# Recurrent block with a routed feed-forward on one core: the second layer norm's aggregate one step later, four dummy products left out, the transpose of h2 behind the expert job

## The chip, the cores and the metric

The kernel runs on one core of one Trainium2 chip. The metric is the device time of one execution in microseconds (us). Three runs of the kernel before took 710.07, 710.91 and 711.07; their median is 710.91.

## The reference, cut to what matters

Eight sequences of 512 tokens with 128 features pass through two blocks.

```python
h = layernorm(x) * (1 + ca) + sa
x = x + ga * mixer(h)          # scan over 512 steps, below
h = layernorm(x) * (1 + cb) + sb
x = x + gb * ffn(h)            # each token goes to the expert with the largest gate

def step(carry, inp):          # mixer
    h_ssm = silu(h_ssm @ A.T + bxt)
    y_ssm = h_ssm @ Cw.T + Cb + dxt
    r = sigmoid(i_r + h_r); z = sigmoid(i_z + h_z); n = tanh(i_n + r * h_n)
    h_rnn = (1.0 - z) * n + z * h_rnn
    y_rnn = h_rnn @ proj_w.T + proj_b
    return (h_ssm, h_rnn), gxt[:, :1] * y_ssm + gxt[:, 1:2] * y_rnn
```

The feed-forward has eight experts, each relu(x @ w1 + b1) @ w2 + b2 with 512 hidden units. All arithmetic is in float32.

## The kernel before

**Tiles and steps.** The 512 steps of the recurrence are cut into 32 tiles c of 16 steps t; a tile holds 16 steps of 8 sequences, so 128 tokens, one per partition. Every engine runs one list of steps g = 16 c + t, and in each of them first its share of the recurrence, then work of other tiles: while the recurrence works on tile c, the engines finish tile c-1 (outputs of the mixer, residual, second layer norm, routing, placing of its rows), prepare tile c+1 (first layer norm, its transpose, the input products), and run expert jobs of earlier groups of tiles. The tiles fall into five groups of 6, 7, 7, 6 and 5; the last tile is done densely. After step 511 there is a tail, in which the engines run the steps of tiles 32 and later without the recurrence.

**The recurrence.** TensorE makes the r product from u (`rs_bank`), then the n and z products from h_ring (`nz_bank`), later in the step the product of the state space and the product of mw for the next step (`carried`, L1297). ScalarE makes r_fac (L787), s_ring (L790), v_fac (L793) and n_fac (L795); VectorE makes the scan (L1122), mw (L1126), u (L1130) and h_ring (L1133). The scan needs r_fac, and r_fac needs u of the step before.

**Around the recurrence.** The step function of VectorE (L1111) puts behind h_ring, in this order: the mixing of tile c-1 at t=2 to 5 (gates, mix, mixg, x), its second layer norm (`post`, L896) from t=6, routing at t=10 to 15, the tables of the dispatch (`lay_out`, L1047, one instruction a step in tiles 7, 14, 21 and 27, t=2 to 11), the first layer norm of a later tile (`pre`, L891), then what leaves the expert jobs' banks: a ReLU of the second hidden bank (L1197) or the addition of the bias into y_sb (L1209); at last the final products. Each engine takes its instructions strictly in order.

**Layer norm in four parts** (L873). Part 0 is bn_stats (L877), part 1 bn_aggr (L880), part 2 xc = (x - mean) * scale (L883), part 3 the result, xc * rstd + shift (L888). Between parts 1 and 3 GpSimd makes rstd in two instructions, an addition of eps (L649) and a power (L651). GpSimd's step function (L701) takes the rstd of the first norm, then at t=6 the rstd of the second norm, then loads of rows for the last group by indirect DMA (L690, at fixed steps; two of them at t=6 of tile 32), then scatters and gathers. `pre_steps` (L253) says at which step the four parts of the first norm run; tiles 1 and 2 have a line of their own there.

**Expert jobs.** A slot is a block of 128 rows of one expert. Its jobs are X (transpose of the rows), A and C (hidden products, chunks 0/1 and 2/3), D and B (output products), each a product of 128 x 128 x 128 in float32. `schedule` (L164) places them by hand-written room: at most `ROOM` = 2 jobs a step, less what `ENDED` and `NEXT` take for tile work. The second of each pair of A and C uses the bank `hid_bank[1]`, whose ReLU is done by VectorE in the step of the job or by ScalarE at the end of it (in the next step for a job in second place).

**TensorE's step** (L1418) is: recurrence products, `tile_work` (L1366; at t=7 the transpose of h1, at t=9 the transpose of h2, which waits for h2), expert jobs, then `hold_clock` (L1311) if there is room, then the state space and `carried`. `hold_clock` is a dummy product of 128 or 256 columns into `hid_bank[1]`, and so waits for every ReLU of that bank that is issued:

```python
ge(eng, relu_b_ready, count_of("AC", u, place))
mm(hid_bank[1][:, 0:width], ident, w_sb[:, W_MOD:W_MOD + width], start=True, stop=True)
```

ScalarE copies the transposes out of PSUM in the step in which TensorE makes them (h1T L736, h2T L817).

**SyncE's queue** loads each slot's expert weights (L583, after reading the expert's number, L582), loads its rows (L589) and stores its results (L600, L597), in the order of the steps.

Of the kernel before, what the change touches and what calls it, by code (L numbers as in the profile page):

```python
# [96 lines left out]
ROOM = 2  # L97
# [8 lines left out]
def taken(u):  # L106

    return (ENDED[u % T] if u >= T else 0) + (NEXT[u % T] if u < (NT - 1) * T else 0)
# [55 lines left out]
def schedule():  # L164

    at, on_act, ready, act_ops, dve_used = {}, set(), {}, {}, {}

    def may(event, u, place):
        return event in ready and ready[event] <= (u, place)

    def ok(unit, u, place, first):
        kind, n, h = unit
        new = n == first
        if kind == "X":
            return new or may(("C", n - 1, 0), u, place)
        if kind == "A":
            return may(("X", n, 0), u, place) and (new or (may(("C", n - 1, h), u, place) and ("D", n - 1, h) in ready))  # L180
        if kind == "C":
            return may(("A", n, h), u, place) and ("A", n, 1) in ready and (new or ("B", n - 1, h) in ready)
        if kind == "D":
            return may(("A", n, h), u, place) and (new or may(("B", n - 1, 1), u, place))
        return may(("C", n, h), u, place) and ("D", n, 1) in ready

    def dve_room(u):
        return 270 if u // T < DVE_EARLY.get(u % T, 0) else DVE_ROOM[u % T]

    def home(unit, u, place):  # L190


        kind, n, h = unit
        if kind == "D" or unit[0::2] == ("B", 0):
            return "PE"
        if (kind == "B" or kind != "X" and h) and dve_used.get(u, 0) + DVE_COST[kind == "B"] <= dve_room(u):
            return "DVE"
        if kind != "B" and act_ops.get(u + (place > 0), 0) < ACT_ROOM[(u + (place > 0)) % T]:
            return "ACT"
        return None  # L200

    u = 0
    for k in range(NG - 1):
        first, end = SLOT0[k], SLOT0[k + 1]
        head = {"X": [], "A": [], "B": [], "C": [], "D": []}
        for unit in order_of_units(k):
            head[unit[0]].append(unit)
        u = max(rows_at(k) + 4, u)
        while any(head.values()) and u < NT * T:
            place = 0  # L210
            while place < ROOM - taken(u):
                for kind in PICK[place > 0]:
                    unit = head[kind][0] if head[kind] else None
                    where = home(unit, u, place) if unit and ok(unit, u, place, first) else None
                    if where:
                        break
                else:
                    break
                head[kind].pop(0)
                at.setdefault(u, []).append(unit)  # L220
                ready[unit] = (u, place + 1)
                if where == "ACT":
                    act_ops[u + (place > 0)] = act_ops.get(u + (place > 0), 0) + 1
                    ready[unit] = (u + (place > 0) + 1, 0)
                    if unit[2]:
                        on_act.add(unit)
                if where == "DVE":
                    dve_used[u] = dve_used.get(u, 0) + DVE_COST[kind == "B"]
                    ready[unit] = (u + 1, 1)
                place += 1  # L230
            u += 1


    def room(u):
        return 3 if u < NT * T + T else 2

    u, used = NT * T, 0
    for k in range(NG):
        if rows_at(k) + 4 > u:
            u, used = rows_at(k) + 4, 0  # L240
        for i, what in enumerate(order_of_units(k)):
            if what in ready:
                continue
            if i == 1:
                u, used = u + 1, 0
            while used >= room(u):
                u, used = u + 1, 0
            at.setdefault(u, []).append(what)
            used += 1
    return at, on_act  # L250


def pre_steps():  # L253

    pre, rstd = {}, {}
    for j in range(1, NT):
        at = (j - 1) * T
        steps = (at + 2, at + 3, at + 5, at + 6) if j < 3 else (at - 7, at - 6, at, at + 1)
        for part, u in enumerate(steps):
            pre.setdefault(u, []).append((j, part))  # L260
        rstd.setdefault(steps[1], []).append(j)
    return pre, rstd


PRE_AT, RSTD_AT = pre_steps()
UNITS, ON_ACT = schedule()
Y_STEP = {SLOT_OF[i]: u for u, what in UNITS.items() for kind, i, second in what
          if kind == "B" and second and i in SLOT_OF}
Y_AT = {u: n for n, u in Y_STEP.items()}
# [28 lines left out]
def adaln_kernel(nc, x, silu_in, weights, ssm_weights, w1, b1, w2, b2, col_bias, bias_a, bias_b,  # L298
                 bias_const, const, out):
    ctx = ExitStack()  # L300
    with ctx:
# [46 lines left out]
        u = sb("u", [P, 2, B])  # L348
# [143 lines left out]
        def exists(tile):  # L492

            return 0 <= tile < NT
# [135 lines left out]
        def _(eng):  # L630
# [70 lines left out]
            def step(u, c, q, t):  # L701

                for tile in RSTD_AT.get(u, []):
                    rstd(tile, mv1, ve1, rs1, ln1_step, ve1_done, rs1_ready)
                if t == 6 and exists(c - 1):
                    rstd(c - 1, mv2, ve2, rs2, ln2_step, ve2_done, rs2_ready)
                for n in range(SLOT0[NG - 1], NSLOT):
                    if u == max(rows_at(NG - 1) + 1, X_STEP[n] - 12):
                        load_rows(n)
                for j in range(NS):  # L710
                    if u == scatter_at(j):
                        ge(eng, h_ready, min(u, NT * T))
                        scatter(j)
                    if u == GATHER_AT[j]:
                        ge(eng, h_ready, min(u, NT * T))
                        gather(j)
# [148 lines left out]
        def _(eng):  # L865
# [30 lines left out]
            def post(j, part):  # L896
                if part == 3 and j >= RING:
                    k = group_of_tile(j - RING)
                    ge(eng, scattered[k % 3], 16 * sum(SIZE[i] for i in range(k % 3, k + 1, 3)))
                layer_norm(j, st2, mv2, rs2, xc2, mod_cb, mod_sb, h2_ring[:, j % RING, :], ln2_step, rs2_ready, h2_ready,  # L900
                           part)
# [209 lines left out]
            def step(g, c, q, t):  # L1111
# [24 lines left out]
                if exists(j):  # L1136
                    xs = x_sb[:, j * P:(j + 1) * P]
                    if t == 2:
                        ge(eng, gates_raw, j + 1)
                        nc.vector.tensor_scalar(g_sb[:, :], g_raw[:, :], 0.5, 0.5, ALU.mult,  # L1140
                                                ALU.add).then_inc(gates_ready, 1)
                    if t == 3:
                        ge(eng, yr_ready, j + 1)
                        nc.vector.scalar_tensor_tensor(out=mix[:, :], in0=work[:, Y_S:Y_S + P],
                                                       scalar=g_sb[:, 0:1], in1=yr_sb[:, :],
                                                       op0=ALU.mult, op1=ALU.add).then_inc(mix_ready, 1)
                    if t == 4:
                        ge(eng, mix_ready, j + 1)
                        nc.vector.tensor_tensor(mixg[:, :], mix[:, :], mod_ga, ALU.mult).then_inc(mixg_done, 1)
                    if t == 5:  # L1150
                        ge(eng, mixg_done, j + 1)
                        nc.vector.tensor_tensor(xs, mixg[:, :], xs, ALU.add).then_inc(x1_ready, 1)
                    if t == 6:
                        ge(eng, x1_ready, j + 1)
                        post(j, 0)
                        post(j, 1)
                    if t in (7, 8):
                        post(j, t - 5)
                    if 10 <= t <= 15:
                        route(j, 1 - q, t)  # L1160
                if c == NT and 5 <= t < 5 + INDEX_STEPS:
# [73 lines left out]
        def _(eng):  # L1235
# [182 lines left out]
            def step(g, c, q, t):  # L1418
# [24 lines left out]
                    mm(z_cols(q, t), wg[:, WG_Z:WG_Z + P] if g else w_sb[:, W_HH + P:W_HH + 2 * P], h_ring[:, pq, pt, :],  # L1443
                       start=False, stop=True, skip_group_check=True).then_inc(z_ready, 1)

                tile_work(c, q, t, g)
                units = UNITS.get(g, [])
                for kind, n, second in units:
                    unit(kind, n, second)
                if exists(c):  # L1450
                    room = ROOM - taken(g) - len(units)
                    if room == 2:
                        hold_clock(g, len(units), 2 * P)
                    if room == 1:
                        hold_clock(g, len(units), P)
                    if g == 0:
                        ge(eng, rn_ready, 2)
                    ge(eng, hs_ready, g)
                    state_space(g, pq, pt).then_inc(s_ready, 1)
                    if exists((g + 1) // T):  # L1460
                        carried(g + 1)
# [56 lines left out]
```

## Time and profile before

| | |
|---|---|
| Median of three runs | 710.91 us |
| Profiled execution | 709.89 us, span 708.0 us |
| TensorE busy, matmul and weight load | 97% and 91% |
| VectorE, ScalarE, GpSimd busy | 76%, 60%, 18% |
| TensorE's mean granted clock | 0.997 |
| Chain that ended last, by engine | TensorE 92%, VectorE 3%, DMA 2% |
| Chain, by output | rs_bank 33%, nz_bank 23%, hid_bank_b 11%, work 11% |

The span runs from the first to the last instruction of the program; the execution's time has some more around it. A busy share counts the time in which at least one instruction of the engine was open; matmuls are pipelined, so TensorE's share says little about how much more it could do. In a timeline each row has the start, the time, the engine, the line, the operation, output and inputs, the shape and a count; like instructions that follow each other are merged; in brackets stands the idle time before the instruction and what ended it. PE is TensorE, DVE VectorE, ACT ScalarE, POOL GpSimd, SP SyncE.

### The profile page before, as it was taken

How to read it: one execution, taken by the hardware profiler on the slowest of the kernel's cores; microseconds unless marked ns; L12 is line 12 of the kernel's file. 1: busy time of each engine (PE TensorE's matmuls, PEld its weight loads, DVE VectorE, ACT ScalarE, POOL GpSimd, SP SyncE). 2: the span in 40 equal slices, each digit the busy share in tenths (PEclk: the TensorE clock that was granted, in tenths of full speed). 3: DMA queues.
4: the chain of work that ended last, by engine and by line, in shares of the span. 5: the costliest groups of instructions: out<-in, count | busy, mean ns of one | idle time of the engine just before them, and what ended most of it. 6: DMA issues, size and time to landing. Idle time of an engine off the chain costs nothing.

```text
span 708.0 us, 35792 instructions
## 1 busy us (share of the span) xinstructions
PE 689.0 (97%) x13884; PEld 646.8 (91%) x13884; DVE 538.9 (76%) x3233; ACT 428.2 (60%) x2678; POOL 127.7 (18%) x221
## 2 busy tenths in 40 slices
PE   8999999999999999999999999999999999998796
PEld 5899999999999999999999999999999999997695
DVE  4777777787787777888887788878787878877465
ACT  4555555556766676566666765766667666664342
POOL 4011111111110111111111112111111112213432
PEclk9999999999999999999999999999999999999999
DMA  8916000604432000063321001632210343224731
GB/s 305 344 60 229 7 7 7 241 9 165 158 118 84 20 15 11 14 229 141 105 84 55 22 19 55 234 137 97 80 38 15 135 165 108 99 100 170 278 123 52
DMA packets 45468, 76.72 MB, mean 108 GB/s; under 512 B 6284, under 2 KB 27090, under 8 KB 45170
## 3 DMA queue, kind: packets, MB, share of 16 engines
q1 hardware_dynamic: 40914, 68.33, 27.0%
q0 software_dynamic: 2368, 4.85, 2.4%
q8 instruction: 110, 1.80, 1.1%
q10 hardware_dynamic: 2016, 1.25, 0.6%
q14 instruction: 60, 0.49, 0.2%
HBM read 14.31 MB, written 21.04 MB: 50 GB/s over the span
## 4 chain that ended last, share of the span: by engine, by line
PE 92%; DVE 3%; DMA 2%; issue 1%; ACT 1%; SPq 1%; POOLq 0%; DVEq 0%
PE rs_bank L1239 33%; PE nz_bank L1239 23%; PE hid_bank_b L1239 11%; PE work L1239 11%; PE y_bank L1239 7%; PE hid_bank_a L1239 7%; DMA yg<-rows,pos 1%; DMA rows<-y_sb 1%; DMA out<-o_sb 0%; SPq L582 0%; DVE u L1130 0%; ACT v_fac L793 0%; DVE mw L1126 0%; DVE y_sb L1209 0%; DVE hid_b L1197 0%
## 5 line engine op out<-in xcount | busy, mean ns | idle before, releaser
L1239 PE MATMUL nz_bank<-h_ring,wg 128*64 128x16 f32 x4088 | 207.2, 211 | 0.0
L787 ACT ACTIVATE r_fac<-rs_bank 128x8 f32<-128x8 f32 x512 | 91.3, 178 | 176.9 <-PE rs_bank L1239 171.2
L1239 PE MATMUL rs_bank<-s_ring,ws_sb 128*64 128x128 f32 x1024 | 195.0, 272 | 0.0
L1239 PEld LDWEIGHTS nz_bank<-h_ring,wg 128*64 128x64 f32 x4088 | 161.1, 136 | 1.3
L1239 PE MATMUL rs_bank<-mw,wg 128*64 128x8 f32 x2044 | 148.5, 202 | 0.0
L1239 PE MATMUL rs_bank<-u,wg 128*64 128x8 f32 x2044 | 142.0, 206 | 0.1
L1122 DVE TENSOR_TENSOR_SCAN nz_bank<-r_fac,nz_bank 128x16 f32<-128x16 f32 x512 | 99.6, 195 | 53.1 <-ACT r_fac L787 33.0
L1239 PEld LDWEIGHTS rs_bank<-s_ring,ws_sb 128*64 128x64 f32 x1024 | 127.3, 136 | 9.2
L1126 DVE SCALAR_TENSOR_TENSOR mw<-v_fac,h_ring 128x8 f32<-128x8 f32 x512 | 85.9, 168 | 54.5
L1239 PEld LDWEIGHTS rs_bank<-mw,wg 128*64 128x64 f32 x2044 | 105.0, 135 | 17.3 <-DVE mw L1126 3.5
L793 ACT ACTIVATE v_fac<-nz_bank 128x8 f32<-128x8 f32 x512 | 90.7, 177 | 40.6
L1239 PEld LDWEIGHTS rs_bank<-u,wg 128*64 128x64 f32 x2044 | 103.1, 135 | 1.4
L1133 DVE SCALAR_TENSOR_TENSOR h_ring<-mw,u 128x8 f32<-128x8 f32 x512 | 85.3, 167 | 17.4
L795 ACT ACTIVATE n_fac<-nz_bank 128x8 f32<-128x8 f32 x512 | 90.7, 177 | 3.1 <-DVE nz_bank L1122 0.6
L1130 DVE SCALAR_TENSOR_TENSOR u<-v_fac,n_fac 128x8 f32<-128x8 f32 x512 | 85.5, 167 | 3.6 <-ACT n_fac L795 0.5
L790 ACT ACTIVATE s_ring<-rs_bank 64x8 f32<-64x8 f32 x512 | 81.0, 158 | 0.4 <-PE rs_bank L1239 0.4
L1239 PE MATMUL hid_bank_b<-w_sb,const_sb 128*64 128x128 f32 (+1 forms) x608 | 76.8, 322 | 2.3 <-ACT hid_b L775 2.3
L665 POOL DMA_INDIRECT rows<-h_ring,pos x31 | 31.7, 1022 | 244.3 <-DVE h_ring L1133 241.6
L779 ACT ACTIVATE hid_a<-hid_bank_a,wx 128x128 f32<-128x128 f32 x132 | 48.5, 368 | 17.6 <-PE hid_bank_a L1239 15.1
L1239 PE MATMUL hid_bank_a<-xT,wx 128*64 128x128 f32 x528 | 55.3, 283 | 0.6 <-issue 0.4
L1239 PE MATMUL hid_bank_b<-xT,wx 128*64 128x128 f32 x528 | 54.4, 280 | 1.3 <-DVE hid_b L1197 1.3
L1239 PE MATMUL y_bank<-wx,hid_a 128*64 128x128 f32 x528 | 54.1, 279 | 0.8 <-DVE y_sb L1209 0.8
(179 smaller groups left out, 1084.6 us busy)
## 6 DMA issues: line engine op xcount, KB each, us to landing
wx<-w_all SPq DMA_DIRECT2D x66, 578.0 KB, 3.9
rows<-zeros SPq DMA_DIRECT2D x3, 4096.0 KB, 14.5
w_all<-in_w SPq DMA_DIRECT2D x2, 2048.0 KB, 15.8
xs_sb<-rows SPq DMA_DIRECT2D x54, 64.0 KB, 2.9
rows<-y_sb SPq DMA_DIRECT2D x54, 64.0 KB, 1.6
x_sb<-in_x SPq DMA_DIRECT2D x1, 1920.0 KB, 9.7
out<-o_sb SPq DMA_DIRECT2D x19, 64.0 KB
out<-o_sb ACTq DMA_DIRECT2D x13, 64.0 KB
```

Source lines behind the costliest of these rows:

```text
L665: nc.gpsimd.indirect_dma_start(rows[k % 3].ap(), index(pos, j), h2_ring[:, j % RING, :], None).then_inc(scattered[k % 3], 16)
L779: nc.scalar.activation(hid_a[:, h, :], hid_bank[0][:, 0:P], ACT.Relu, bias=bias1(i, 2 * h)).then_inc(relu_a_ready, 1)
L787: nc.scalar.activation(r_fac[:, k, :, 1], r_cols(q, t), ACT.Tanh, scale=0.5).then_inc(rn_ready, 1)
L790: nc.scalar.activation(s_ring[0:SSM, pq, pt, 0:B], s_cols(g - 1), ACT.Silu).then_inc(hs_ready, 1)
L793: nc.scalar.activation(v_fac[:, k, :], z_cols(q, t), ACT.Tanh, scale=-0.5).then_inc(sig_ready, 1)
L795: nc.scalar.activation(n_fac[:, k, :], n_pairs(q, t)[:, :, 1], ACT.Tanh).then_inc(tanh_ready, 1)
L1122: nc.vector.tensor_tensor_scan(pairs, r_fac[:, k, :, :].rearrange("p b k -> p (b k)"), pairs, 0.0, ALU.mult, ALU.add).then_inc(pre_n_ready, 1)
L1126: nc.vector.scalar_tensor_tensor(out=mw[:, k, :], in0=v_fac[:, k, :], scalar=1.0, in1=h_ring[:, pq, pt, :], op0=ALU.subtract, op1=ALU.mult ...
L1130: nc.vector.scalar_tensor_tensor(out=u[:, k, :], in0=v_fac[:, k, :], scalar=1.0, in1=n_fac[:, k, :], op0=ALU.add, op1=ALU.mult).then_inc(u ...
L1133: nc.vector.scalar_tensor_tensor(out=h_ring[:, q, t, :], in0=mw[:, k, :], scalar=-0.5, in1=u[:, k, :], op0=ALU.mult, op1=ALU.add).then_inc ...
L1239: last = nc.tensor.matmul(out[c:c + COLS], weights[:, c:c + COLS], moving, start=start, stop=stop, skip_group_check=skip_group_check)
```

## The change

The second layer norm's bn_aggr moves from t=6 to t=7, where xc already stands, and GpSimd's rstd of that norm from t=6 to t=7. `schedule` also returns the set of steps at which a ReLU of the second hidden bank is open, and in these steps TensorE makes no dummy product. At t=9 the expert jobs come ahead of `tile_work`, that is of the transpose of h2. The last two parts of the first layer norm of tiles 1 and 2 run one step earlier.

```diff
@@ schedule
+                if kind in "AC" and unit[2]:
+                    relu_open.update(range(u, ready[unit][0] + ready[unit][1]))
...
-    return at, on_act
+    return at, on_act, relu_open
@@ pre_steps
-        steps = (at + 2, at + 3, at + 5, at + 6) if j < 3 else (at - 7, at - 6, at, at + 1)
+        steps = (at + 2, at + 3, at + 4, at + 5) if j < 3 else (at - 7, at - 6, at, at + 1)
@@ GpSimd, step
-                if t == 6 and exists(c - 1):
+                if t == 7 and exists(c - 1):
                     rstd(c - 1, mv2, ve2, rs2, ln2_step, ve2_done, rs2_ready)
@@ VectorE, step
                     if t == 6:
                         ge(eng, x1_ready, j + 1)
                         post(j, 0)
+                    if t == 7:
                         post(j, 1)
-                    if t in (7, 8):
-                        post(j, t - 5)
+                        post(j, 2)
+                    if t == 8:
+                        post(j, 3)
@@ TensorE, step
-                tile_work(c, q, t, g)
+                if t != 9:
+                    tile_work(c, q, t, g)
                 units = UNITS.get(g, [])
                 for kind, n, second in units:
                     unit(kind, n, second)
+                if t == 9:
+                    tile_work(c, q, t, g)
                 if exists(c):
-                    room = ROOM - taken(g) - len(units)
+                    room = 0 if g in RELU_OPEN else ROOM - taken(g) - len(units)
```

## Rows read from the trace of the kernel before

**Rows 1.** All h_ring writes (L1133): count, min/median/max ns, first and last start.

```profile
L1133 DVE SCALAR_TENSOR_TENSOR h_ring<-mw,u x512: 166/166/170, 12.2 to 639.0; 128x8 f32<-128x8 f32 x171
```

**Rows 2.** Timeline of VectorE, tile 9, t=6 to t=9: start us, us, line, operation.

```profile
195.17 0.17 DVE L1133 SCALAR_TENSOR_TENSOR h_ring<-mw,u 128x8 f32<-128x8 f32 x1
...
195.57 0.18 DVE L880 BATCH_NORM_AGGREGATE mv<-st 128x2 f32<-128x6 f32 x1
195.67 0.32 DVE L1197 TENSOR_SCALAR hid_b<-hid_bank_b,wx 128x128 f32<-128x128 f32 x1
195.91 0.18 DVE L1122 TENSOR_TENSOR_SCAN nz_bank<-r_fac,nz_bank 128x16 f32<-128x16 f32 x1
...
196.53 0.17 DVE L1133 SCALAR_TENSOR_TENSOR h_ring<-mw,u 128x8 f32<-128x8 f32 x1
...
197.74 0.17 DVE L1133 SCALAR_TENSOR_TENSOR h_ring<-mw,u 128x8 f32<-128x8 f32 x1
197.83 0.35 DVE L888 SCALAR_TENSOR_TENSOR h_ring<-xc,rs,mod 128x128 f32<-128x128 f32 x1
...
198.95 0.17 DVE L1133 SCALAR_TENSOR_TENSOR h_ring<-mw,u 128x8 f32<-128x8 f32 x1
...
199.23 0.34 DVE L1197 TENSOR_SCALAR hid_b<-hid_bank_b,wx 128x128 f32<-128x128 f32 x1
...
200.19 0.17 DVE L1133 SCALAR_TENSOR_TENSOR h_ring<-mw,u 128x8 f32<-128x8 f32 x1
```

**Rows 3.** Waits, whole span: engine and line, waited for: us, times, longest.

```profile
PE hid_bank_b L1239 <- ACT hid_b L775: 2.3, 4, 0.8
```

**Rows 4.** Timeline of VectorE, tile 11, t=6 and t=7.

```profile
234.26 0.17 DVE L1133 SCALAR_TENSOR_TENSOR h_ring<-mw,u 128x8 f32<-128x8 f32 x1
...
235.57 0.17 DVE L1133 SCALAR_TENSOR_TENSOR h_ring<-mw,u 128x8 f32<-128x8 f32 x1
...
237.38 0.17 DVE L1133 SCALAR_TENSOR_TENSOR h_ring<-mw,u 128x8 f32<-128x8 f32 x1
```

**Rows 5.** Timeline of VectorE, tile 31, t=9.

```profile
631.68 0.17 DVE L1133 SCALAR_TENSOR_TENSOR h_ring<-mw,u 128x8 f32<-128x8 f32 x1
...
632.96 0.17 DVE L1133 SCALAR_TENSOR_TENSOR h_ring<-mw,u 128x8 f32<-128x8 f32 x1
```

**Rows 6.** Timeline of VectorE, tile 7, t=7.

```profile
157.86 0.26 DVE L1068 TENSOR_TENSOR ended<-passed,end_slot 128x104 f32<-128x104 f32 x1
```

**Rows 7.** Timeline of GpSimd, tile 9, t=6.

```profile
195.84 0.18 POOL L649 TENSOR_TENSOR ve<-mv,eps 128x1 f32<-128x1 f32 x1 [2.82 <-DVE mv L880]
196.10 0.57 POOL L651 TENSOR_TENSOR rs<-ve,half 128x1 f32<-128x1 f32 x1
```

**Rows 8.** Timeline of GpSimd, tile 1, t=6.

```profile
40.22 0.26 POOL L649 TENSOR_TENSOR ve<-mv,eps 128x1 f32<-128x1 f32 x1 [2.89 <-DVE mv L880]
```

**Rows 9.** Timeline of TensorE, tile 9, t=9.

```profile
198.23 0.44 PE L1239 MATMUL work<-const_sb,h_ring 128*64 128x128 f32 x4
```

**Rows 10.** Timeline of ScalarE, tile 9, t=10.

```profile
199.34 0.18 ACT L787 ACTIVATE r_fac<-rs_bank 128x8 f32<-128x8 f32 x1 [0.36 <-PE rs_bank L1239]
```

**Rows 11.** Timeline of VectorE, tile 1, t=6 and the end of t=7.

```profile
39.55 0.17 DVE L1133 SCALAR_TENSOR_TENSOR h_ring<-mw,u 128x8 f32<-128x8 f32 x1
...
42.50 0.17 DVE L1133 SCALAR_TENSOR_TENSOR h_ring<-mw,u 128x8 f32<-128x8 f32 x1
```

**Rows 12.** Timeline of GpSimd, tile 32, t=6.

```profile
649.00 0.94 POOL L690 DMA_INDIRECT xs_sb<-rows,x_index  x1 [0.30 <-issue]
```

**Rows 13.** Timeline of VectorE, tile 32, t=13.

```profile
653.07 0.28 DVE L1209 TENSOR_TENSOR y_sb<-y_bank,wx 128x128 f32<-128x128 f32 x1
```

**Rows 14.** Timeline of SyncE's queue, tail.

```profile
655.38 0.52 SPq L600 DMA_DIRECT2D rows<-y_sb  x1
```

**Rows 15.** Timeline of TensorE, tail.

```profile
667.86 0.44 PE L1239 MATMUL rs_bank<-const_sb,xs_sb 128*64 128x128 f32 x4 [3.53 <-DMA xs_sb<-rows,x_index]
```

**Rows 16.** Stretch: its us, each engine's busy us, TensorE's granted clock, DMA.

```profile
669.40:672.80 3.40, 3.40 (x36) 3.40 (x34) 0.87 (x4) 1.00 (x3) 2.49 (x4) 0.51 0.94 345
```

More of the change, by code:

```diff
@@ L164, in schedule @@
 def schedule():
-    at, on_act, ready, act_ops, dve_used = {}, set(), {}, {}, {}
+    at, on_act, ready, act_ops, dve_used, relu_open = {}, set(), {}, {}, {}, set()
     def may(event, u, place):
@@ L265 @@
 PRE_AT, RSTD_AT = pre_steps()
-UNITS, ON_ACT = schedule()
+UNITS, ON_ACT, RELU_OPEN = schedule()
 Y_STEP = {SLOT_OF[i]: u for u, what in UNITS.items() for kind, i, second in what
```

## The prediction

> **What bounds the kernel.** I read the page first, and its TensorE share (in the table above) is misleading: dummy products fill that engine. What sets the time is a recurrence of 512 steps, each of which writes one h_ring. The row of all h_ring writes puts them between 12.2 and 639.0 us [rows 1]: 626.8 us for 511 steps, 1.227 us each. So the second view is the timeline of VectorE around single steps. There the reader is to see the distance from one h_ring to the next: 197.74 to 198.95 is 1.21 us, 196.53 to 197.74 is 1.21 us [rows 2], and I take 1.205 as the floor. 511 floors are 615.8 us, so 11.0 us of the recurrence is excess, and that is all that the change can win before the tail (the last 69 us, behind the last h_ring). I then looked for which steps hold the excess. Step numbers t run from 0 to 15 in each of 32 tiles c; a distance is put to the step that begins it.
>
> At **t=6** VectorE has bn_stats, bn_aggr and, in many tiles, one more instruction between h_ring and the next scan. In tile 9 the scan starts at 195.91, 0.74 behind h_ring at 195.17, and the step takes 1.36 [rows 2]; without that 0.155 of excess it would start 0.58 behind. That is the free window of a step. At **t=7** of four tiles TensorE's dummy product waits for the ReLU that still reads its bank: 2.3 us in four waits, the longest 0.8 [rows 3]; the step takes 1.81 (235.57 to 237.38) [rows 4]. At **t=9** each step is a little long: 1.24 in tile 9 [rows 2], 1.28 in tile 31 [rows 5].
>
> **The change part by part.**
>
> *The dummy products.* The set of steps with an open ReLU has 149 members, but only four of them still had room for a dummy: t=7 of tiles 11, 18, 25 and 31. The other 148 dummies stay. Each of three steps returns 1.81 - 1.205 = 0.605. The fourth dummy is twice as wide and its wait is 0.8 where the others leave (2.3 - 0.8)/3 = 0.5, so I take 0.9. Sum 3 x 0.605 + 0.9 = **-2.7 us**. What is late next: ScalarE's ReLU and the copy of h1's transpose, which it has in other tiles' t=7 in the same number at 1.21 (tile 9 [rows 2]). So nothing is left of the stall, and at worst 0.1 in each.
>
> *The aggregate leaves t=6.* It starts 0.40 behind h_ring (195.57) and the ReLU 0.50 (195.67); without it the ReLU can start 0.28 behind, as behind bn_stats at t=9 (199.23 against 198.95) [rows 2]. ReLU to scan is 0.24 (195.67 to 195.91), so the scan is free at 0.52, inside 0.58. Eight tiles have a ReLU there: 8 x 0.155 = **-1.24**. Eight have the y_sb addition instead, at 1.31 (234.26 to 235.57) [rows 4]: 8 x 0.105 = **-0.84**. The other tiles from 2 to 31 lose nothing there today, but for the four with a table step of the dispatch (7, 14, 21, 27), for which I take 0.1 each.
>
> *The aggregate arrives at t=7.* There stands only xc. The aggregate starts 0.09 behind h_ring and takes 0.18; xc needs its result and starts at 0.30; the scan is free 0.24 to 0.28 later, at 0.54 to 0.58. This just fits: 0 taken, and 0.05 in each of 31 tiles as the bad end. In the four dispatch tiles the table product stands behind xc, 0.26 long [rows 6]. Its cost lies between 0 and 0.26; I take 0.2, nearer to the row, since the window is full. Four times 0.1 - 0.2 is **+0.4**.
>
> *The reciprocal root on GpSimd.* It follows the aggregate, which now comes 0.9 later (1.205 + 0.09 - 0.40). Its two instructions run from 195.84 to 196.67 [rows 7], 0.92 behind the aggregate's end (195.75). From t=7 that is 0.27 + 0.92 = 1.19 behind h_ring, and h2 wants it at 1.205 + 0.09 = 1.295 (it starts 0.09 behind its h_ring, 197.83 against 197.74). It is hidden, with 0.1 to spare. But the first of the two now lies beside xc, and where it lay beside another such product, in tile 1, it took 0.26 and not 0.18 [rows 8]. Then h2 starts some 0.03 late, which only the tiles without work ahead of the transpose feel: **+0.2** in all. The Trainium skill, GPSIMD Engine Reference, section Key points, says that GpSimd shares its SBUF interfaces with VectorE and contends with instructions of two SBUF inputs, as xc is; that speaks against this move, and by that the trace agrees. By the rule the sum is as it stands; if rule and row did not hold it would be 0.2 better.
>
> *The transpose behind the expert job at t=9.* h2 ends at 197.83 + 0.35 = 198.18 and the transposes start at 198.23 [rows 9]: TensorE waits for h2, and r_fac of the next step is late with it. With a job of four such products first (0.44 with its drain, as this row), the wait is covered. 22 of the tiles 8 to 31 have a job at t=9; 14 and 21 have none and keep theirs, as do 1 to 7. Five tiles return 1.24 - 1.205, seventeen 1.28 - 1.205 (from tile 13 on h2 has one more wait): **-1.45**. What moves with it: ScalarE's copy of the transpose, and what it does behind it; ScalarE idles 0.36 before r_fac at 199.34 [rows 10], nearly a whole job, and a job's start-to-start is less than its 0.44, so I take no cost. The bounds are 0 (ScalarE takes the place of the wait) and -1.45.
>
> *First layer norm of tiles 1 and 2.* Its last two parts come one step sooner, so TensorE finds h1 ready at t=7, and t=6 is relieved. In tile 1 t=6 and t=7 take 42.50 - 39.55 = 2.95 [rows 11], 0.54 over two floors. Tile 0 has the same pair, and I take as much: **-1.08**. The parts arrive at t=4 and t=5 beside one other 128x128 instruction, and two fit (0.28 + 0.24).
>
> *The tail.* One queue is passed: on GpSimd the two loads of rows of step t=6 of tile 32 now stand ahead of the root, each 0.94 with 0.30 before it [rows 12], 2.5 us at most. They start before the root's old turn, so I take 1.6 of it for h2 of the last tile, and for VectorE, which waits for the root in order with all that is queued behind; the two loads come sooner. I cost this at nothing, for two covers. SyncE stores the y_sb of 653.07 [rows 13] only at 655.38 [rows 14], its queue being behind: 653.07 + 0.28 + 1.6 is still ahead of that. And TensorE waits 3.53 us for rows at 667.86 [rows 15], which are gated by that queue and not by h2. With the covers gone it costs 1.6.
>
> Sum: -2.7 - 1.24 - 0.84 + 0.4 + 0.2 - 1.45 - 1.08 = **-6.7 us**, of the 11.0. The profiled execution took 709.89 (span 708.0 and 1.9 around it), so 703.2; the median shown, 710.91, is 1.0 above it, so **704.2**.
>
> **The rivals.**
>
> *The tail gains.* Today's wait of 3.53 is followed by the granted clock at 0.51 from 669.40 to 672.80 [rows 16], the lower level, 1.2 GHz, for 3.4 us: 1.7 us lost. If the late h2 pushes 1.5 us of TensorE's work into that wait, 2.0 are left of it, and no row shows whether 2.0 is enough to lower the clock. If not, 704.2 - 1.7 = 702.5. The Trainium skill, TensorE: Matmul & The Clock Gate, section on the HAM clock gate, says that recent activity sets the clock; by that the gain is possible, and the trace agrees as far as it goes.
>
> *t=7 is the new t=6.* Aggregate and xc overfill it by 0.05 in 31 tiles: 1.55, so 705.75; for it speaks that the fit above has no slack, against it that the aggregate is short.
>
> *The root is late, and the kernel slower.* h2 can slip from 0.09 to 0.58 - 0.26 = 0.32 before it holds the scan of t=8. Past that, each 0.1 costs 31 x 0.1 = 3.1, and from 0.22 past it the kernel is slower than before. With both instructions at twice their length (0.75 more) it would be 0.75 - 0.10 - 0.23 = 0.42 past: 13.0, so 717.2. Against it: the contention seen is 0.08.
>
> *Half of it does nothing.* If t=6 and t=9 are long for another reason (TensorE's own work), only the dummies and tiles 0 and 1 count, -3.8, with the losses of 0.6: 707.7. Against it: the scans at t=6 stand right behind VectorE's own instructions.
>
> **How the numbers follow.** Forecast 0.52, tail gain 0.20, overfull t=7 0.20, the half case 0.04, the late root 0.04 (0.01 of it within 0.2% of before). The range takes in the forecast, the tail gain with 0.5 of its unknowns (702.0) and the overfull t=7 with half of the t=9 term missing (706.4). 0.2% (1.4 us) is about what a measurement of this kernel can tell from no change: faster 0.96, the same 0.01, slower 0.03.
>
> **What would show it.** Right: no wait of a dummy for a ReLU; steps t=6 and t=7 at 1.205 in tiles like 9 and 11, t=7 at 1.4 in the four dispatch tiles; t=9 at 1.205 in tiles with a job; the last h_ring near 632.3. Wrong: scans behind xc later than 0.58 after h_ring, h2 later than 0.12, or a tail longer than 69 us.

## The result and the profile after

The changed kernel took 703.26 us in the median of four runs (701.33 to 703.70), against 710.99 of before: a ratio of 0.9885, 95% interval 0.9866 to 0.9903. Five runs more gave 702.04 (experiment e8). The forecast was 704.2, the range 702.0 to 706.4. The profiled execution took 701.33 (span 699.5), 8.6 less than the profiled one of before.

The page of the changed kernel gives the busy times and the chain; TensorE has 16 records less than before (13884), four for each of the four dummy products, and its share of the chain is 94%:

```profile
PE 683.9 (98%) x13868; PEld 641.9 (92%) x13868; DVE 536.6 (77%) x3233; ACT 426.1 (61%) x2678; POOL 129.0 (18%) x221
...
PE 94%; DMA 2%; DVE 1%; issue 1%; POOL 0%; SPq 0%; ACT 0%; POOLq 0%; DVEq 0%
```

The row of all h_ring writes, which stands against [rows 1]:

```profile
L1135 DVE SCALAR_TENSOR_TENSOR h_ring<-mw,u x512: 166/166/170, 11.6 to 632.4; 128x8 f32<-128x8 f32 x171
```

The last h_ring comes at 632.4 and not at 639.0, 6.6 us sooner. Of that 0.5 is the start (11.6 and not 12.2, before the change acts), so 6.1 are the recurrence. The other 2.0 are the tail: 699.5 - 632.4 = 67.1, before 708.0 - 639.0 = 69.0.

VectorE in tile 9, t=6 to t=9, against [rows 2]:

```profile
193.76 0.17 DVE L1135 SCALAR_TENSOR_TENSOR h_ring<-mw,u 128x8 f32<-128x8 f32 x1
...
194.04 0.33 DVE L1201 TENSOR_SCALAR hid_b<-hid_bank_b,wx 128x128 f32<-128x128 f32 x1
194.32 0.19 DVE L1124 TENSOR_TENSOR_SCAN nz_bank<-r_fac,nz_bank 128x16 f32<-128x16 f32 x1
...
194.96 0.17 DVE L1135 SCALAR_TENSOR_TENSOR h_ring<-mw,u 128x8 f32<-128x8 f32 x1
195.05 0.17 DVE L882 BATCH_NORM_AGGREGATE mv<-st 128x2 f32<-128x6 f32 x1
195.25 0.35 DVE L885 SCALAR_TENSOR_TENSOR xc<-x_sb,mv,mod 128x128 f32<-128x128 f32 x1
195.53 0.20 DVE L1124 TENSOR_TENSOR_SCAN nz_bank<-r_fac,nz_bank 128x16 f32<-128x16 f32 x1
...
196.17 0.17 DVE L1135 SCALAR_TENSOR_TENSOR h_ring<-mw,u 128x8 f32<-128x8 f32 x1
196.41 0.35 DVE L890 SCALAR_TENSOR_TENSOR h_ring<-xc,rs,mod 128x128 f32<-128x128 f32 x1
196.68 0.28 DVE L1213 TENSOR_TENSOR y_sb<-y_bank,wx 128x128 f32<-128x128 f32 x1
196.88 0.18 DVE L1124 TENSOR_TENSOR_SCAN nz_bank<-r_fac,nz_bank 128x16 f32<-128x16 f32 x1
...
197.51 0.17 DVE L1135 SCALAR_TENSOR_TENSOR h_ring<-mw,u 128x8 f32<-128x8 f32 x1
...
198.71 0.17 DVE L1135 SCALAR_TENSOR_TENSOR h_ring<-mw,u 128x8 f32<-128x8 f32 x1
```

At t=6 the ReLU starts 0.28 behind h_ring, as forecast, the scan 0.56 (forecast 0.52, and free up to 0.58), and the step takes 1.20 (1.36 before). At t=7 aggregate, xc and scan start 0.09, 0.29 and 0.57 behind; the step takes 1.21. At t=9, behind a job, 1.20 (1.24 before). But t=8 takes 1.34 and took 1.21: h2 starts 0.24 behind its h_ring and not 0.09, the y_sb addition comes behind it, and the scan only 0.71 behind. Tile 11's t=7, against [rows 4], is 1.20, and no dummy's wait for a ReLU [rows 3] is left; tile 7's t=7, a dispatch tile, is 1.40:

```profile
233.78 0.17 DVE L1135 SCALAR_TENSOR_TENSOR h_ring<-mw,u 128x8 f32<-128x8 f32 x1
...
234.98 0.17 DVE L1135 SCALAR_TENSOR_TENSOR h_ring<-mw,u 128x8 f32<-128x8 f32 x1
```

```profile
156.03 0.17 DVE L1135 SCALAR_TENSOR_TENSOR h_ring<-mw,u 128x8 f32<-128x8 f32 x1
...
156.63 0.25 DVE L1070 TENSOR_TENSOR ended<-passed,end_slot 128x104 f32<-128x104 f32 x1
156.81 0.18 DVE L1124 TENSOR_TENSOR_SCAN nz_bank<-r_fac,nz_bank 128x16 f32<-128x16 f32 x1
...
157.43 0.17 DVE L1135 SCALAR_TENSOR_TENSOR h_ring<-mw,u 128x8 f32<-128x8 f32 x1
```

Why h2 was late in tile 9 stands on GpSimd, against [rows 7]; below it tile 8, with its xc on VectorE in the second fence:

```profile
175.99 0.18 POOL L651 TENSOR_TENSOR ve<-mv,eps 128x1 f32<-128x1 f32 x1 [3.77 <-DVE mv L882]
176.25 0.57 POOL L653 TENSOR_TENSOR rs<-ve,half 128x1 f32<-128x1 f32 x1
...
195.31 0.34 POOL L651 TENSOR_TENSOR ve<-mv,eps 128x1 f32<-128x1 f32 x1 [3.69 <-DVE mv L882]
195.73 0.57 POOL L653 TENSOR_TENSOR rs<-ve,half 128x1 f32<-128x1 f32 x1
```

```profile
175.93 0.38 DVE L885 SCALAR_TENSOR_TENSOR xc<-x_sb,mv,mod 128x128 f32<-128x128 f32 x1
```

In tile 9 the addition of eps took 0.34 and xc 0.35; in tile 8, at the same place in the step, the addition took 0.18 and xc 0.38. Every tile shows one of the two. I call a root behind an addition of 0.34 a late root; in this execution tiles 3, 6, 9, 10, 11 and 29 have one. Tiles 3 and 6, with no job at t=9, lose 0.16 there, tiles 9 and 29, with a y_sb at t=8, lose 0.13 and 0.15; 10 and 11 lose nothing, since the job ahead of the transpose covers it.

In the tail TensorE's wait for rows, against [rows 15], is 0.78 and not 3.53, and its granted clock from 663.0 to 669.0 is 1.00, the 2.4 GHz level, where it was 0.51 behind the wait [rows 16]. The first fence has the wait, the second the stretch: its length, busy times, clock:

```profile
660.71 0.44 PE L1243 MATMUL rs_bank<-const_sb,xs_sb 128*64 128x128 f32 x4 [0.78 <-DMA xs_sb<-rows,x_index]
```

```profile
663.00:669.00 6.00, 6.00 (x107) 5.54 (x104) 3.72 (x13) 2.68 (x9) 4.67 (x5) 1.00 0.84 284
```

### The profile page after: what moved, and what is told of

Same layout as the page of the kernel before. It is cut to its first block, busy times and chain, and to the rows that moved or that the text cites. A ratio compares the mean times of both kernels' runs of the same rounds, so it can differ in the third digit from the quotient of the medians.

```text
span 699.5 us, 35760 instructions
## 1 busy us (share of the span) xinstructions
PE 683.9 (98%) x13868; PEld 641.9 (92%) x13868; DVE 536.6 (77%) x3233; ACT 426.1 (61%) x2678; POOL 129.0 (18%) x221
## 3 DMA queue, kind: packets, MB, share of 16 engines
q10 hardware_dynamic: 2016, 1.25, 0.6%
## 4 chain that ended last, share of the span: by engine, by line
PE 94%; DMA 2%; DVE 1%; issue 1%; POOL 0%; SPq 0%; ACT 0%; POOLq 0%; DVEq 0%
PE rs_bank L1243 34%; PE nz_bank L1243 23%; PE hid_bank_b L1243 12%; PE work L1243 11%; PE y_bank L1243 8%; PE hid_bank_a L1243 7%; DMA xs_sb<-rows,x_index 1%; DMA rows<-y_sb 1%; DMA out<-o_sb 1%; DVE fin_g L1219 0%; POOL xs_sb L692 0%; DVE hid_b L1201 0%; POOL yg L681 0%; SPq L584 0%; DVE prob L1014 0%
## 5 line engine op out<-in xcount | busy, mean ns | idle before, releaser
L1243 PE MATMUL rs_bank<-mw,wg 128*64 128x8 f32 x2044 | 146.4, 202 | 0.0
L1243 PE MATMUL rs_bank<-u,wg 128*64 128x8 f32 x2044 | 140.0, 206 | 0.1
L1243 PEld LDWEIGHTS rs_bank<-mw,wg 128*64 128x64 f32 x2044 | 103.0, 135 | 18.6 <-DVE mw L1128 4.3
L1243 PE MATMUL hid_bank_b<-w_sb,const_sb 128*64 128x128 f32 (+1 forms) x592 | 74.8, 322 | 0.0
```

The costliest lines, as they stand in the source:

```text
L1243: last = nc.tensor.matmul(out[c:c + COLS], weights[:, c:c + COLS], moving, start=start, stop=stop, skip_group_check=skip_group_check)
```

## The experiments

All were timed against the kernel before on the same chip; its median was 710.35 in e1 to e4, 710.24 in e5 to e8, 710.80 in e9 to e11 and 710.45 in e12. From e5 on each account opens with the median in us, the range of the runs, and the ratio to before with its 95% interval. Steps, last h_ring and tail are read from the one profiled execution of each kernel.

### The four parts, each alone on the kernel before

```diff
e1  +                    room = 0 if g in RELU_OPEN else ROOM - taken(g) - len(units)
e2  +                if t == 7 and exists(c - 1): rstd(c - 1, mv2, ...)      # GpSimd
    +                    if t == 7: post(j, 1); post(j, 2)                  # VectorE
e3  +                if t == 9: tile_work(c, q, t, g)                       # behind the units
e4  +        steps = (at + 2, at + 3, at + 4, at + 5) if j < 3 else ...
```

> The kernel before with the four dummy products left out and nothing else. Theory (the terms of the change add up): t=7 of tiles 11, 18, 25 and 31 falls to about 1.21 us, the last h_ring comes 2.6 us sooner, the tail stays at 69.0 us, the time falls by 2.6 us (ratio 0.9963). Rival (the dummies held TensorE's clock or only hid a wait of the ReLU itself): less than 1.5 us, with t=7 of these tiles above 1.4 us. Rival for the tail (its 2.0 us gain belongs to the phase in which the tail begins, not to one part): the tail is shorter than 68 us here too.

> The kernel before with the second norm's aggregate and its reciprocal root moved to t=7, and nothing else. Theory (the root behind two loads of rows shortens the tail; the second product against GpSimd's addition costs some tiles): t=6 gives 2.5 us, t=7 of the four dispatch tiles takes back 0.8, six tiles with a late root (ve 0.34 and not 0.18 us long) take back about 0.9, so the last h_ring comes 0.8 us sooner; the tail falls from 69.0 to about 67 us; together 2.8 us less (ratio 0.996). Rival (the tail's gain is not of this part): tail 69.0 us, together 0.8 us less (ratio 0.999). Rival for the late roots (they come with the other parts): no ve longer than 0.20 us in tiles 2 to 31, 1.7 us less in the recurrence.

> The kernel before with the expert jobs ahead of the transpose at t=9, and nothing else. Theory (terms add up): t=9 of 22 tiles falls from 1.24 to 1.28 us to about 1.21 us, the last h_ring comes 1.25 us sooner, the tail stays at 69.0 us, the time falls by 1.25 us (ratio 0.998). Rival (ScalarE's copy of the transpose takes the place of the wait): t=9 stays above 1.23 us in these tiles, under 0.4 us in all.

> The kernel before with the last two parts of the first layer norm of tiles 1 and 2 one step sooner, and nothing else. Theory: t=6 and t=7 of tiles 0 and 1 fall by 1.0 us in all, but for what the aggregate at t=6 costs in tile 1 (0.15), so 0.9 us; nothing later changes, tail 69.0 us (ratio 0.9987). Rival (the pair of steps is long because of the aggregate alone): under 0.4 us.

| | median us | range us | ratio | last h_ring | tail |
|---|---|---|---|---|---|
| e1 dummies | 707.58 | 706.31 to 709.64 | 0.9965 [0.9953, 0.9977] | 635.7 | 70.9 |
| e2 aggregate | 707.90 | 705.88 to 712.78 | 0.9972 [0.9956, 0.9989] | 639.9 | 71.1 |
| e3 transpose | 708.57 | 705.54 to 709.69 | 0.9972 [0.9960, 0.9984] | 637.5 | 69.8 |
| e4 first norm | 709.33 | 708.28 to 710.34 | 0.9984 [0.9975, 0.9994] | 636.7 | 70.7 |

(The last two columns are of the profiled execution.) In e1 the four steps return 0.61, 0.61, 0.61 and 0.82, 2.66 together. In e3 t=9 falls by 1.17 in all, in e4 t=6 and t=7 of tiles 0 and 1 by 1.02. In the steps that they touch these three parts are what they were expected to be, and their rivals fall. In medians the four parts alone gain 2.77, 2.45, 1.78 and 1.02 us, 8.0 together, against 7.7 and 8.2 for the whole change. No tail is shorter than 69 in the four profiled executions, but one execution each does not tell whose part the tail's gain is: e2, for one, has five runs of twelve with a mean clock above 0.997, which no run of before has.

e2 is the odd one. Its profiled execution took 712.78, longer than before: t=6 gave 2.7 and t=7 took 0.75, but t=8 and t=9 took 3.0 more. 25 tiles had the long addition, 19 of them a late h2. Tile 2 in e2 (GpSimd at t=7, VectorE from t=7 to the end of t=9):

```profile
60.10 0.34 POOL L649 TENSOR_TENSOR ve<-mv,eps 128x1 f32<-128x1 f32 x1 [3.46 <-DVE mv L880]
60.52 0.57 POOL L651 TENSOR_TENSOR rs<-ve,half 128x1 f32<-128x1 f32 x1
```

```profile
59.75 0.17 DVE L1133 SCALAR_TENSOR_TENSOR h_ring<-mw,u 128x8 f32<-128x8 f32 x1
60.05 0.35 DVE L883 SCALAR_TENSOR_TENSOR xc<-x_sb,mv,mod 128x128 f32<-128x128 f32 x1
...
60.96 0.17 DVE L1133 SCALAR_TENSOR_TENSOR h_ring<-mw,u 128x8 f32<-128x8 f32 x1
61.21 0.35 DVE L888 SCALAR_TENSOR_TENSOR h_ring<-xc,rs,mod 128x128 f32<-128x128 f32 x1
...
62.17 0.17 DVE L1133 SCALAR_TENSOR_TENSOR h_ring<-mw,u 128x8 f32<-128x8 f32 x1
...
63.57 0.17 DVE L1133 SCALAR_TENSOR_TENSOR h_ring<-mw,u 128x8 f32<-128x8 f32 x1
```

h2 starts 0.25 behind, and t=9 takes 1.40. The twelve runs lie 6.9 us apart (e4's 2.1). The late root is not fixed to tiles: here it falls on 25, in the changed kernel's profile on six, and e8 shows others for that same kernel. In the whole change e3's part hides most of what e2's part costs.

### The late root

e5 and e6 leave out the addition and take the root straight from the variance, so GpSimd has one instruction (and the output differs); e9 makes the addition twice; e8 is the changed kernel unaltered.

```diff
e5 on the changed kernel, e6 on e2:
+                if mv is mv2:
+                    nc.gpsimd.tensor_tensor(rs, mv[:, 1:2], half, ALU.pow); return
e9 on the changed kernel:
+                    nc.gpsimd.tensor_tensor(rs, mv[:, 1:2], eps, ALU.add)
                     nc.gpsimd.tensor_tensor(ve, mv[:, 1:2], eps, ALU.add)
                     nc.gpsimd.tensor_tensor(rs, ve, half, ALU.pow)
```

> The changed kernel, with the root of the second norm taken straight from the variance: GpSimd's addition of eps is left out (the output differs by that). Theory (the late roots come from this addition beside xc): no h2 starts later than 0.13 us behind its h_ring, t=9 of tiles 3 and 6 and t=8 of tiles 9 and 29 return to 1.205 to 1.25 us, the recurrence is 0.6 us shorter than in the profiled execution of the changed kernel. Rival (any instruction of GpSimd beside xc is lengthened, so the power instead): the power takes 0.73 us and not 0.57, xc 0.35, h2 still starts in time since the root ends at about 1.1 us, so the same time, but the power shows the contention. Rival (the late h2 has another cause): some h2 at 0.24 us or more.

> The kernel before with the aggregate and the root moved to t=7 as in e2, and the addition of eps left out for the second norm. Theory (late roots make e2's loss at t=8 and t=9 and its spread of 6.9 us between executions): t=8 and t=9 as before (1.205 and 1.24 to 1.28 us), so the recurrence is 1.9 us shorter than before instead of 1.5 longer; the runs lie within 3.5 us of each other, and their median is at least 0.5 us under e2's 707.9. Rival (the spread comes from the tail): a spread of 6 us or more here too, with all h2 in time.

> The changed kernel once more, unaltered, to see what differs between executions. Theory (two things differ: which tiles have a late root, and how long the tail's wait for rows is): the steps t=6 and t=7 are the same within 0.02 us in every tile, the tiles with ve of 0.34 us are others than 3, 6, 9, 10, 11 and 29, the tail lies between 67 and 71 us, the runs lie 3 us apart. Rival: the same six tiles again, and a tail of 67.1 us.

> The changed kernel with GpSimd's addition of eps made twice for the second norm, the first time into rs. The root ends 0.26 us later, at 1.44 us behind the h_ring of t=7 or at 1.60 where the addition beside xc is long, so h2 starts at about 0.33 to 0.50 us in every tile. Theory (past 0.32 us h2 holds the scan of t=8, and each 0.1 us past it costs that in the tile): t=8 is 0.05 to 0.20 us longer in all tiles, t=9 0.24 us longer in the nine tiles without a job, the recurrence 3 to 6 us longer. Rival (a late root is hidden but at the transpose and y_sb): t=8 is 1.205 us but in tiles 9, 16, 23 and 29, the recurrence 1.5 to 3 us longer.

**e5**: 700.25 (699.67 to 702.49), 0.9866 [0.9849, 0.9883]. No h2 is late, and the four steps return to between 1.21 and 1.25. Yet its first rival is right about the contention: the power, now beside xc, is the one that is long. The two rows of e5's roots, first norm and second (count, min/median/max ns):

```profile
L656 POOL TENSOR_TENSOR rs<-ve,half x32: 550/552/672, 6.4 to 588.0; 128x1 f32<-128x1 f32 x32
L652 POOL TENSOR_TENSOR rs<-mv,half x32: 549/725/732, 39.9 to 642.3; 128x1 f32<-128x1 f32 x32
```

The first norm's power takes 0.55, the second's, beside xc, 0.73 in most tiles. It is the overlap that costs, not the addition; without the addition the root is early enough to bear it. The 0.6 us expected shows at t=8 and t=9 (0.53 less, and 0.25 less at t=7), but 0.7 more, spread thinly over all other steps, leaves the recurrence of this execution as it was. In medians e5 lies 1.8 under the unaltered kernel of the same rounds (e8).

**e6**: 706.49 (705.59 to 710.43), 0.9959 [0.9945, 0.9973]. t=8 and t=9 are as before to 0.03 us in all, the recurrence is 1.5 shorter where e2's was 1.5 longer, and the median is 1.4 under e2's. So e2 lost its time by the late roots. The spread, 4.8, lies between the 3.5 of the theory and the 6 of the rival: part of it is not the late roots'.

**e8**: 702.04 (701.86 to 704.67), 0.9896 [0.9879, 0.9913]. t=6 and t=7 are as in the first execution to 0.03, and 17 tiles have the long addition, of which only 6, 10, 11 and 29 had it before; tail 67.4. So the tiles differ by execution.

**e9**: 711.26 (710.52 to 713.53), 1.0012 [1.0001, 1.0022]. Tile 2 in e9, t=7 to t=9: the root is late enough to hold the scan:

```profile
59.06 0.17 DVE L1142 SCALAR_TENSOR_TENSOR h_ring<-mw,u 128x8 f32<-128x8 f32 x1
59.35 0.35 DVE L892 SCALAR_TENSOR_TENSOR xc<-x_sb,mv,mod 128x128 f32<-128x128 f32 x1
...
60.27 0.17 DVE L1142 SCALAR_TENSOR_TENSOR h_ring<-mw,u 128x8 f32<-128x8 f32 x1
60.79 0.35 DVE L897 SCALAR_TENSOR_TENSOR h_ring<-xc,rs,mod 128x128 f32<-128x128 f32 x1 [0.35 <-POOL rs L656]
61.06 0.18 DVE L1131 TENSOR_TENSOR_SCAN nz_bank<-r_fac,nz_bank 128x16 f32<-128x16 f32 x1
...
61.69 0.17 DVE L1142 SCALAR_TENSOR_TENSOR h_ring<-mw,u 128x8 f32<-128x8 f32 x1
```

h2 starts 0.52 behind its h_ring and t=8 takes 1.42, 0.22 more. In tiles 25 and 31, where h2 starts 0.41 and 0.42, it is 0.11 more. Both give the same point from which h2 costs one for one: 0.52 - 0.22 = 0.30. The price was right; how many tiles pay it was put too low (t=8 and t=9 cost 8.7 us where 3 to 6 were expected), since in 26 of 31 tiles the addition beside xc was long here.

### The tail

```diff
e7 on the changed kernel, GpSimd (VectorE's aggregate alike):
+                if t == (6 if c == NT else 7) and exists(c - 1): rstd(c - 1, mv2, ...)
e10 on the changed kernel:
+                    room = ROOM - taken(g) - len(units)
```

> The changed kernel, with the aggregate and the root of the last tile back at t=6, ahead of the two loads of rows. Theory (the root behind the loads shortens the tail): the wait for rows is 3.5 us or longer, the clock drops behind it, the tail is 69 us or longer, no run has a mean clock over 0.997, the time is 1.5 us above the changed kernel's. Rival (the tail's length is set by when the rows land, which differs between executions): tail between 67 and 71 us, a time within 0.5 us of the changed kernel's.

> The changed kernel with the four dummy products back. Theory (terms add up): t=7 of tiles 11, 18, 25 and 31 returns to 1.82 and 2.03 us, the last h_ring comes 2.6 us later. For the tail, theory: its length goes with the moment at which it begins and not with one part of the change (all kernels whose last h_ring was at 633 us or sooner had SyncE's store of y_sb 10.95 us behind it issued in 0.53 us, all others in 1.09 us or more), so with the last h_ring at 635 us this store takes 1.09 us or more, the tail 69 us or more, the time is 4 us above the changed kernel's. Rival: the store takes 0.53 us, the tail stays at 67 us, the time is 2.6 us above.

**e7**: 701.48 (700.83 to 701.85), 0.9878 [0.9862, 0.9893], tail 66.4, mean clocks 0.998 and 0.999 in all four runs. The root ahead of the loads does not bring the long tail back; the theory falls. **e10**: 707.72 (703.62 to 708.30), 0.9949 [0.9931, 0.9966]. t=7 of the four tiles is back at 1.81 to 2.03, 2.6 together. The store took 1.57, the tail 66.3: neither side. That execution was the fastest of six, though; four took 707.6 to 708.3, so that the median is 5.7 above e8's, more than either side expected, and no trace is kept of those four. e9's tail of 68.0 from 641.0, and e6's 66.9 from 637.0, also speak against the moment as what sets the tail. What holds in all fourteen profiled executions is the wait for rows: under 1.6 us in all where the tail is 68.0 or less, 3.3 to 4.7 where it is 69.0 or more.

### A version that gains more

```diff
e11 on the changed kernel:
+def aggregate_step(c):            # 7 where VectorE has a ReLU or y_sb at t=6, else 6
+                if exists(c - 1) and t == aggregate_step(c): rstd(c - 1, mv2, ...)
+                hold_clock(...)   # at t=9 ahead of tile_work
e12 on e11, GpSimd:
-                    if u == max(rows_at(NG - 1) + 1, X_STEP[n] - 12):
+                    if u == max(rows_at(NG - 1) + 1, X_STEP[n] - (16 if n == 58 else 12)):
```

> The changed kernel, with the aggregate and the root of the second norm at t=7 only in tiles where VectorE has a ReLU or a y_sb at t=6, and at t=9 the dummy product too ahead of the transpose. Theory: t=7 of tiles 7, 14 and 27 returns to 1.205 us against 0.05 to 0.09 us more at t=6 (0.3 us in all), no late root in tiles without a job at t=9, and their t=9 falls from 1.25 and 1.28 to 1.21 us (0.4 us), and the late roots at t=9 no longer cost 0.3 us: the last h_ring comes 1.0 us sooner than with the change, the time is 1.0 us less than the changed kernel's median of 702.0. Rival (ScalarE's copy then holds r_fac, or the dummy is too long for the step): t=9 of these tiles stays above 1.24 us, and the time is within 0.5 us of the changed kernel's.

> The selective kernel (e11) with one load of rows in the tail, that of slot 58, issued four steps sooner, so that on GpSimd it stands ahead of the gather of tile 20 and no longer behind it. In all executions so far the tail was 66.3 to 68.0 us where TensorE waited under 1.5 us for these rows, and 69.0 to 71.1 us where it waited 3.3 us or more. Theory (the wait comes from GpSimd's gather, which waits for SyncE's stores, and the load queued behind it): TensorE does not wait over 0.5 us for these rows, the tail is 66 to 67 us, all mean clocks are 0.998 or 0.999, the runs lie within 2 us of each other with a median near 700.5. Rival (the DMA engines are full in this stretch, so another load or the weights are late instead): a wait of 1 us or more of TensorE for other rows or weights between 25 and 35 us behind the last h_ring, tails over 68 us still, a median near 702.

**e11**: 702.64 (701.24 to 703.57), 0.9877 [0.9860, 0.9893]. t=7 of tiles 7, 14 and 27 returns to 1.21 (0.58 less, against 0.22 more at t=6), and t=9 of the nine tiles without a job falls to 1.21: 0.74 less, 0.40 of it in tiles 3 and 6. Their rival falls, but the time does not show it: two late roots more at t=8 (0.3), one long step of tile 6 (t=11, 1.56; 1.21 in the changed kernel and 1.33 in the kernel before) and 0.5 spread thinly over the other steps took it back in the recurrence, and the tail is 69.1. Here are the row of the wait and the stretches of it and behind it:

```profile
661.69 0.44 PE L1251 MATMUL rs_bank<-const_sb,xs_sb 128*64 128x128 f32 x4 [3.32 <-DMA xs_sb<-rows,x_index]
```

```profile
658.30:661.60 3.30, 0.07 (x2) 0.00 (x0) 1.10 (x4) 0.00 (x0) 2.39 (x4) 1.00 0.81 273
663.20:666.60 3.40, 3.40 (x38) 3.40 (x36) 1.21 (x4) 1.00 (x3) 2.48 (x4) 0.52 0.88 321
```

After a wait of 3.3 the granted clock is 0.52, the lower level, for the 3.4 us of the second row. On GpSimd the load of these rows stands right behind the tail's first gather. It is issued at 656.33 and lands 5.3 us later, when TensorE's wait ends:

```profile
655.08 0.95 POOL L688 DMA_INDIRECT yg<-rows,pos  x1 [9.07 <-issue]
656.33 0.95 POOL L699 DMA_INDIRECT xs_sb<-rows,x_index  x1 [0.30 <-DMA y_rows<-y_sb]
```

The kernel lets that gather wait for SyncE's stores. The row names no store, but the chain that ended last in the changed kernel does (start, us, what):

```profile
651.00 3.57 DMA rows<-y_sb
...
655.61 0.79 POOL yg L681
...
656.86 3.80 DMA xs_sb<-rows,x_index
```

**e12** takes one load, slot 58's, from behind the first gather of the tail: 699.21 (698.88 to 700.41), 0.9852 [0.9835, 0.9868], the fastest of all. GpSimd and TensorE in its tail:

```profile
644.93 0.94 POOL L699 DMA_INDIRECT xs_sb<-rows,x_index  x1 [0.30 <-issue]
653.96 0.95 POOL L688 DMA_INDIRECT yg<-rows,pos  x1 [8.08 <-issue]
```

```profile
656.82 0.39 PE L1251 MATMUL rs_bank<-const_sb,xs_sb 128*64 128x128 f32 x4
658.75 0.44 PE L1251 MATMUL hid_bank_b<-h2T,w_all 128*64 128x128 f32 x4 [1.32 <-DVE hid_b L1209]
```

The load is out 9 us before the gather, TensorE no longer waits for these rows, and the tail is 65.9. So the load's place behind the gather is what lets these rows come late. It is not what makes the wait long in one execution and short in another: e7 and e11 issue this load 23.8 us behind the last h_ring, and it lands 2.8 us later in e7 and 5.3 in e11. What delays the landing is open. Of the 4.6 us between the profiled executions of e11 and e12 the tail has 3.3; the recurrence has 1.1, with five late roots where e11 had fifteen. Two of the four mean clocks are 0.997, not 0.998, and a wait of 1.3 for hid_b stands where the rows were awaited; the rival's long tail did not show.

## Why the prediction was right

**The dummies**: -2.7 forecast, -2.66 alone (e1). The wait was the whole of the excess.

**t=6**: the ReLU tiles return 0.16 each (0.155), the y_sb tiles 0.09 to 0.10 (0.105) but for tile 18 (0.05). **The dispatch tiles** gain 0.04 to 0.21 at t=6 and lose 0.19 to 0.20 at t=7: net +0.34 for a forecast of +0.4. The bound of 0 to 0.26 was rightly read from its row.

**t=7 "just fits"**: it does, to 0.015 us. Where xc takes 0.38, t=7 takes 1.22, else 1.207; some 0.3 in all. The rival of an overfull step (1.55) named the right place and far too large a size. The rival by which t=6 and t=9 give nothing falls with e2's t=6 and with e3.

**First norm**: -1.08 forecast, -1.01. **Transposes**: -1.45 forecast, -1.2 (e3: -1.17); seven tiles (12, 19, 23, 26, 27, 28, 31) stay at 1.22 to 1.23. In these ScalarE has a ReLU behind the copy, and r_fac starts right behind that, with no idle time. So ScalarE took 0.02 of the wait in each of the seven, where no cost was taken; in the others it did not take the place of the wait.

**The root, +0.2**: this term was mis-sized, and its bearer missed. I took 0.08 for the contention, from the one row that showed it [rows 8]; it is 0.16, and h2 slips to 0.24 and not 0.12. The "0.1 to spare" was wrong too. The root's end was put at 1.19 behind h_ring, and with a short addition it is there (1.18); but from its end to the start of h2 go another 0.11, which the sum left out (tile 9: 195.73 + 0.57 = 196.30, h2 at 196.41). That makes 1.29 of the 1.295 there are: nothing was to spare, and all of the 0.16 reaches h2. (By the prediction's own figures, 1.19 + 0.08, h2 would not have been late at all; its 0.03 does not follow from them.) The late root falls on a number of tiles that differs between executions, and on t=8 of the tiles with a y_sb there, not only on the transposes without a job. In the profiled execution it cost 0.6 (0.33 at t=9, 0.28 at t=8). By the Trainium skill, GPSIMD Engine Reference, section Key points, GpSimd contends with instructions of VectorE that have two SBUF inputs, as xc has; the trace agrees, and adds that either may pay: xc 0.03, or GpSimd 0.16 to 0.18. By the prediction's own sign (h2 later than 0.12) this step was wrong. Had every tile had it, only 1 to 6 at t=9 and four at t=8 would pay (6 x 0.16 + 4 x 0.14 = 1.5): the t=9 edit covers the rest. That interplay the sum did not see: it priced the two edits apart.

**The late root as a rival** gave 0.32 as the point from which h2 costs one for one; e9 measures 0.30, and with it the kernel is indeed no faster than before.

**The tail, 0**: mis-sized, by 2.0 in the profiled execution. The rival of a gain had the right sign, place and size (wait shortened, no lower clock behind it). Its mechanism holds in part: with the last tile's h2 late, TensorE comes to these rows 27.5 us behind the last h_ring (their product starts at 28.3, less its wait of 0.8) and not 25.3 (28.9 less 3.5), so less of the wait is left. But that is neither needed nor enough. In e7, where h2 is not late, TensorE comes at 25.8 and the wait is 0.9, since the rows are there at 26.7; in e2, where h2 is late, it comes at 27.6 and waits 3.6, since they are there at 31.2. The landing of the rows decides, and e12 shows what gives it room: the load ahead of the gather on GpSimd. Open is why the change makes the short tail more likely. The mean clock of the runs without a trace is a rough sign of it (the changed kernel's profiled execution has a short tail and 0.997): none of the 73 runs of before beside the experiments had a mean clock above 0.997, four of the changed kernel's nine and all of e7's had, as had e2's in 5 of 12, e3's in 1, and 14 of the 41 of e5, e6 and e9 to e12.

The sum of the recurrence, -6.7, stands against -6.1 of the steps; the start's 0.5 and the tail's 2.0 came on top in that execution, and the medians, 703.26 and 702.04, lie between that execution and the forecast. That the medians came within 0.9 and 2.2 us of the forecast is in part luck: a recurrence 0.6 short of the sum and a tail put at nothing work against each other.

## What to carry to other kernels

Before moving an instruction, list what it will run beside on the other engines at its new place, and price the overlap on either engine at its longest, not at the one overlap that the old trace happens to show. Price edits that touch one chain together: here one edit made h2 late and another made its lateness free. When an end-to-end gain varies by more than the terms, compare the waits of several executions before giving the gain to a part.

## What was not expected of the hardware

An overlap of GpSimd's 128x1 addition with VectorE's 128x128 xc ends in one of two ways, at starts equal to a few nanoseconds: xc takes 0.38 and the addition 0.18, or xc takes 0.35 and the addition 0.34. Which it is changes from tile to tile and from execution to execution. In the kernel before, where the addition stood at t=6, none was over 0.28.

In the second way the addition ends 0.05 behind xc's end (tile 9: 195.31 + 0.34 = 195.65, against 195.25 + 0.35 = 195.60): it looks as if it waited for xc. The Trainium skill, SBUF — State Buffer, section SBUF: two separate sides, calls the shared ports an exclusive lock, which the instruction that starts first keeps to its end. The second way agrees with that. The first does not: in tile 8 xc starts 0.06 ahead of the addition too (175.93 and 175.99), and the addition is through at 176.17, before xc's end at 176.31. What decides between them stays open.
